# A decoder's latent attention: ScalarE copies each group of turned probabilities one step later

## Chip, cores and metric

The kernel runs on one core of one Trainium2 chip. The metric is the device time of one execution in microseconds (us); less is better. Engines: TensorE (PE; its weight loads are PEld), VectorE (DVE), ScalarE (ACT), GpSimd (POOL) and SyncE (SP), each with its own queue of instructions, worked in order; they wait for each other by semaphores only.

## What is computed

Two decoder layers on x of 4 x 256 x 256, each of self-attention, cross-attention to a context of 4 x 1601 x 64 and a mixture of experts, with a layer norm behind each. The change is in the second layer's cross-attention ("latent block"), 16 heads on a rotated context:

```python
q_hk = (hidden_q @ Wq.T).reshape(Bv, Sv, H, K)
q_big = jnp.einsum('bshk,hkq->bshq', q_hk, w_kc_q)
q_big = _apply_rope(q_big, ...)            # 192 wide
kv_r = _apply_rope(kv_c, ...)              # 1601 x 64
q_r = jnp.einsum('bshq,hqr->bhsr', q_big, W_qr)
k_r = jnp.einsum('bld,hdr->bhlr', kv_r, W_kr)
scores = jnp.einsum('bhsr,bhlr->bhsl', q_r, k_r)
attn = jax.nn.softmax(scores, axis=-1)
ctx_c = jnp.einsum('bhsl,bld->bhsd', attn, kv_r)
ctx_lat = jnp.einsum('bhsd,hkd->bhsk', ctx_c, w_kc_kv)
out = ctx_lat.transpose(0, 2, 1, 3).reshape(Bv, Sv, H * K) @ Wo.T
```

## The kernel before

`latent_attention` (L2426) works on 64 units, one for each head and batch. A unit has 256 queries in two halves of 128 rows, and 1601 keys. Products keep float32 accuracy by splitting an operand into a `_hi` part (ScalarE rounds it to fp32r) and a `_lo` part (VectorE subtracts `_hi` from the source).

For a unit u the work is:

- `score(u, i, j)`: TensorE scores half i against piece j of the keys (304, 496, 496 and 305 wide) into PSUM bank j. It waits until the exponential of the score before it in that bank is done.
- `maximum(u, i, j)`: VectorE reduces each piece; with the fourth it combines the four (L2698) to the row maximum `e_st`.
- `exponential(u, i, j)`: ScalarE, with sum, to `e_P` (L2631). It waits for the combined maximum of its half.
- `turn(u, g)`: TensorE transposes group g of up to 256 keys (seven groups, the last of 65 keys) from `e_P` into one of two banks. It waits until the lower half of group g - 2 has been taken out.
- `upper_pt(u, g)` on ScalarE (L2646, `e_PT_hi`) and `lower_pt(u, g)` on VectorE (L2713, `e_PT_lo`): the two halves of the turned group. The lower one waits for the upper one. These are the copies of the change.
- `attend(u, g)`: TensorE multiplies both halves by the context. `keep_context` (L2638, `e_cx_hi`) copies the result, VectorE its lower half; `project_out` gives the output.

The units are pipelined. Iteration i has eight steps; in step s the engines do, for u = i: score, maximum and exponential of (u, half 1, piece s) or, from step 4 on, of the next unit's half 0 (ScalarE's exponentials lag by half a unit: steps 0 to 3 are half 0 of u, steps 4 to 7 half 1); for v = i - 1: `turn(v, s)`, the two copies of group s, and `attend(v, s - 3)`. The order on each queue is written out by hand in loops over i and step: `tensor` (L2583), `scalar` (L2653), `vector` (L2740). Beside these, in fixed steps: the queries of the next unit are absorbed into the keys' space (`absorb_q`, TensorE step 1; `upper_qk` on ScalarE step 2, L2624, `e_qk_hi`); queries are projected (`project_q`, step 3; ScalarE copies them to `x_in` in step 4, L2314, GpSimd rotates them, ScalarE's `upper_z` copies them in step 7, L2320); and in three of four iterations weights of the next head are folded (`fold_q`, `fold_r`, `fold_o`: TensorE step 5, ScalarE's copy step 6, L2298, L2304 or L2308, VectorE's lower half step 6).

`score_bank` are banks 0 to 3, `tb_bank` (turned groups) 4 and 5, the context has 6, all the rest shares bank 7 (`aux`). There are four `e_PT` buffers, used in turn. In `scalar`, the copy stands at the end of each step:

```python
if v is not None and step < GROUPS:
    upper_pt(v, step)
```

Of the kernel before, what the change touches and what calls it, by code (L numbers as in the profile page):

```python
# [54 lines left out]
def decoder(nc, t, out):  # L55
    with ExitStack() as top:
# [159 lines left out]
        def norm_scalar(turns, b, k):  # L216
            act.wait_ge(xt_turned, turns)
            act.copy(XT_hi[:, :, tok(b)], turned_view(k)).then_inc(xt_hi, 1)
# [20 lines left out]
        def scaled_scalar(turns, b, k, at):  # L239
            act.wait_ge(ln_in, 16)  # L240
            act.wait_ge(xt_turned, turns)
            for c in range(DC):
                last = act.activation(XT_hi[:, c, tok(b)], turned_view(k)[:, c, :], ACT.Copy, scale=ln_w[:, at + c:at + c + 1])
            last.then_inc(xt_hi, 1)
# [60 lines left out]
        def enter_scalar(b):  # L305
            act.wait_ge(x_normed, 16 + b + 1)
            act.copy(x_in[:, 2 * b:2 * b + 2, :], X[:, 2 * b:2 * b + 2, :]).then_inc(x_entered, 1)
# [2118 lines left out]
        def latent_attention(latent, before, following):  # L2426
# [8 lines left out]
            GROUPS = -(-KT // 2)  # L2435
# [6 lines left out]
            with ExitStack() as sc:  # L2442
# [20 lines left out]
                def a_unit(i):  # L2463
                    return i if 0 <= i < N else None
# [5 lines left out]
                def keys_of(g):  # L2470

                    return min(2, KT - 2 * g), min(P, CTX - 2 * g * P)
# [141 lines left out]
                def scalar():  # L2614
                    def upper_o(h):
                        if h >= 2:
                            act.wait_ge(*put_out.at(BATCH * (h - 1)))
                        latent.upper_o(h, bank[aux])

                    def upper_qk(m):  # L2620
                        act.wait_ge(*q_absorbed.at(m + 1))
                        if m >= 2:
                            act.wait_ge(*scored.at(8 * (m - 1)))
                        act.copy(qk[m % 2][0][:], bank[aux][:, 0:SEQ]).then_inc(*qk_hi.up())  # L2624

                    def exponential(u, i, j):
                        if i == 0 and j == 0 and u >= 2:
                            act.wait_ge(*turned.at(GROUPS * (u - 1)))
                        act.wait_ge(*maxed.at(2 * u + i + 1))
                        n, s = PIECES[j], st[u % 4]  # L2630
                        act.activation(Pm[u % 2][:, i, STARTS[j]:STARTS[j] + n], bank[score_bank[j]][:, 0:n], ACT.Exp,  # L2631
                                       bias=s[:, i, 4:5], accum_out=s[:, i, j:j + 1]).then_inc(*exped.up())

                    def keep_context(u):
                        act.wait_ge(*attended.at(GROUPS * (u + 1)))
                        if u >= 2:
                            act.wait_ge(*put_out.at(u - 1))
                        act.copy(cx[u % 2][0][:], bank[ctx_bank][:, 0:SEQ]).then_inc(*cx_hi.up())  # L2638

                    def upper_pt(u, g):  # L2640
                        at = GROUPS * u + g
                        n, rows = keys_of(g)
                        act.wait_ge(*turned.at(at + 1))
                        if at >= PT_BUFS:
                            act.wait_ge(*attended.at(at - PT_BUFS + 1))
                        act.copy(PT[at % PT_BUFS][0][0:rows, 0:n, :],  # L2646
                                 bank[tb_bank[at % 2]][0:rows, 0:n * SEQ].rearrange("p (c n) -> p c n", c=n)).then_inc(*pt_hi.up())

                    act.wait_ge(*before)
                    upper_qk(0)  # L2650
                    upper_o(0)
                    latent.upper_z(1)
                    for i in range(N + 3):  # L2653
                        u, v, w, after = a_unit(i), a_unit(i - 1), a_unit(i - 2), a_unit(i + 1)
                        h, quarter = i // BATCH + 1, i % BATCH
                        for step in range(8):
                            half, j = divmod(step, 4)
                            if u is not None:
                                exponential(u, half, j)
                            if step == LAG - 1 and w is not None:  # L2660
                                keep_context(w)
                            if step == 2 and after is not None:
                                upper_qk(after)
                            if step == 4 and i + 2 < N:
                                latent.keep_q(i + 2, bank[aux])
                            if step == 1 and i == N:
                                enter_scalar(0)
                            if step == 6 and h < H and quarter < 3:
                                if quarter == 0:
                                    latent.upper_q(h, bank[aux])  # L2670
                                elif quarter == 1:
                                    latent.upper_r(h, bank[aux])
                                else:
                                    upper_o(h)
                            if v is not None and step < GROUPS:
                                upper_pt(v, step)
                            if step == 3 and i + 2 == BATCH - 1:
                                norm_scalar(12 + BATCH, BATCH - 1, aux)
                            if step == 2 and i == N:
                                scaled_scalar(16 + 1, 0, enter_bank, 0)  # L2680
                            if step == 7 and i + 2 < N:
                                latent.upper_z(i + 2)
# [108 lines left out]
                sync()  # L2791
                tensor()
                scalar()
                vector()
                gpsimd()
# [166 lines left out]
```

## Time and profile before

| | |
|---|---|
| time, median of 3 runs | 1911.38 us (1908.85 to 1916.75) |
| the profiled execution | 1909.03 us, its span 1907.8 us |
| latent block | about 785 to 1600 us of the span |
| TensorE busy, share of the span | 1775.6 us, 93% |
| VectorE, ScalarE, GpSimd busy | 1289.9 (68%), 1086.8 (57%), 685.6 us (36%) |

The span is the time from the first to the last instruction that the profiler saw. Busy time is the time in which an engine had an instruction at work; TensorE's matmuls overlap, so full busy time doesn't mean full throughput. A timeline row gives start, duration, engine, source line, operation, output and inputs; a bracket at its end gives the idle time ahead of it and what ended that. Consecutive instructions of an engine overlap a little, so the distance between starts is shorter than a duration.

### The profile page before, as it was taken

Reading aid. Unit: us, or ns where it says so; the run is one execution under the profiler, and the core shown is the slowest. Engines: PE = TensorE matmul, PEld = TensorE weight load, DVE = VectorE, ACT = ScalarE, POOL = GpSimd, SP = SyncE. Lnnn points to the kernel's source line nnn. Section 1 sums busy time; section 2 is a strip of 40 time slices with the busy share of each in tenths; the row PEclk is TensorE's granted clock in tenths of the full one; section 3 lists DMA queues with packets and bytes.
Section 4 is the critical chain, followed back from the end, with each engine's and each line's share of the span. In section 5 each row is a group of like instructions: output and inputs, shape, how many; then the busy total and the mean of one; then the engine's idle time right before and its main releaser. Section 6 shows DMA issues by size and latency. Waiting matters only on the chain.

```text
span 1907.8 us, 41954 instructions
## 1 busy us (share of the span) xinstructions
PE 1775.6 (93%) x15624; PEld 1478.5 (77%) x15624; DVE 1289.9 (68%) x3463; ACT 1086.8 (57%) x2750; POOL 685.6 (36%) x674
## 2 busy tenths in 40 slices
PE   7999989889998898699999999999999998898995
PEld 5999977646656776599999999999999997774663
DVE  5677657732237665588888888888888888775222
ACT  5776754212223343488888888888888885431221
POOL 5644322232224422443444334433443341213221
PEclk9999999989999999999999999999999999999998
DMA  4000039023247000000000000000000002402323
GB/s 167 23 1 2 1 131 344 23 87 48 45 101 222 3 3 2 22 12 12 12 12 12 29 12 12 12 12 12 12 12 1 1 2 84 193 2 82 48 46 66
DMA packets 51861, 91.69 MB, mean 48 GB/s; under 512 B 4592, under 2 KB 43632, under 8 KB 49232
## 3 DMA queue, kind: packets, MB, share of 16 engines
q1 hardware_dynamic: 42928, 78.16, 12.3%
q0 software_dynamic: 8160, 10.29, 3.5%
q8 instruction: 129, 2.11, 0.5%
q10 hardware_dynamic: 576, 0.56, 0.1%
q14 instruction: 68, 0.56, 0.1%
HBM read 56.13 MB, written 32.87 MB: 47 GB/s over the span
## 4 chain that ended last, share of the span: by engine, by line
PE 73%; DVE 12%; ACT 6%; issue 3%; POOL 2%; DMA 2%; SPq 0%; ACTq 0%; DVEq 0%; POOLq 0%
PE bank L100 60%; PE bank L2546 10%; DVE a_t L703 2%; ACT d_PT L1338 2%; ACT landing L1338 1%; PE bank L1887 1%; PE bank L1159 1%; DVE a_t L700 1%; PE bank L1866 1%; POOL c_rows L1767 1%; POOL g_rows L1767 1%; DVE tiny L133 1%; PE bank L501 1%; DVE d_nm L1426 1%; DVE X L172 0%
## 5 line engine op out<-in xcount | busy, mean ns | idle before, releaser
L2694 DVE TENSOR_REDUCE e_st<-bank 128x1 f32<-128x496 f32 (+2 forms) x512 | 292.0, 571 | 121.7 <-PE bank L100 120.7
L2631 ACT ACTIVATE e_P<-bank,e_st 128x496 f32<-128x496 f32 (+2 forms) x512 | 307.0, 600 | 95.3 <-DVE e_st L2698 93.5
L2713 DVE TENSOR_TENSOR e_PT_lo<-bank,e_PT_hi 128x512 fp32r<-128x512 f32 (+1 forms) x448 | 287.6, 642 | 1.5 <-ACT e_PT_hi L2646 1.4
L2546 PE MATMUL bank<-ident,e_P 128*128 128x128 f32 (+1 forms) x1664 | 258.4, 274 | 4.2 <-DVE e_PT_lo L2713 3.7
L2646 ACT CAST e_PT_hi<-bank 128x512 fp32r<-128x512 f32 (+1 forms) x448 | 248.3, 554 | 10.9 <-PE bank L2546 6.7
L100 PE MATMUL bank<-e_PT_hi,e_kv 128*128 128x256 f32 (+1 forms) x832 | 249.2, 320 | 0.0
L2546 PEld LDWEIGHTS bank<-ident,e_P 128*128 128x128 f32 (+1 forms) x1664 | 195.0, 140 | 31.3 <-issue 26.5
L100 PE MATMUL bank<-e_PT_lo,e_kv 128*128 128x256 f32 (+1 forms) x832 | 215.6, 280 | 0.0
L100 PE MATMUL bank<-e_KT,e_qk_hi 128*128 128x496 f32 (+2 forms) x512 | 198.9, 389 | 7.2 <-ACT e_P L2631 5.7
L100 PE MATMUL bank<-e_KT,e_qk_lo 128*128 128x496 f32 (+2 forms) x512 | 177.0, 346 | 0.0
L100 PEld LDWEIGHTS bank<-e_PT_lo,e_kv 128*128 128x128 f32 (+1 forms) x832 | 158.4, 190 | 2.5
L100 PEld LDWEIGHTS bank<-e_PT_hi,e_kv 128*128 128x128 f32 (+1 forms) x832 | 157.6, 189 | 2.2
L2393 POOL TENSOR_TENSOR e_r<-x_in,e_ropeq 96x512 f32<-96x512 f32 x32 | 41.1, 1284 | 217.5 <-ACT x_in L2314 217.5
L100 PEld LDWEIGHTS bank<-e_KT,e_qk_hi 128*128 128x128 f32 x512 | 95.9, 187 | 29.6 <-ACT e_P L2631 20.1
L2393 POOL TENSOR_TENSOR x_in<-x_in,e_ropeq 96x512 f32<-96x512 f32 x32 | 41.0, 1282 | 205.2 <-ACT x_in L2314 205.2
L100 PE MATMUL bank<-mask_b,ident_b 128*128 128x128 bf16 (+1 forms) x796 | 100.8, 274 | 11.4 <-DVE d_nm L1428 6.9
L2631 ACT ACTIVATION_READ_ACCUMULATOR e_P<-bank,e_st 128x1 f32 x512 | 102.5, 200 | 0.0
L1531 POOL TENSOR_SCALAR_AFFINE_SELECT landing<-landing 128x768 f32<-128x768 f32 x64 | 39.5, 640 | 167.5 <-ACT landing L1338 167.5
L100 PEld LDWEIGHTS bank<-e_KT,e_qk_lo 128*128 128x128 f32 x512 | 96.9, 189 | 0.1
L1338 ACT ACTIVATE d_PT<-bank 128x1536 f32<-128x1536 f32 x32 | 46.4, 1451 | 86.7 <-PE bank L100 86.7
L100 PEld LDWEIGHTS bank<-mask_b,ident_b 128*128 128x128 bf16 x796 | 58.5, 99 | 44.0 <-DVE d_nm L1428 8.6
L1338 ACT ACTIVATE landing<-bank 128x1536 f32<-128x1536 f32 x32 | 46.4, 1450 | 80.7 <-PE bank L100 80.7
(470 smaller groups left out, 4960.1 us busy)
## 6 DMA issues: line engine op xcount, KB each, us to landing
c_wall<-in_c_w SPq DMA_DIRECT2D x8, 1536.0 KB, 19.0
g_wall<-in_g_w SPq DMA_DIRECT2D x8, 1536.0 KB, 19.4
c_rows<-normed SPq DMA_DIRECT2D x9, 1040.0 KB, 12.9
g_rows<-normed SPq DMA_DIRECT2D x9, 1040.0 KB, 13.1
e_stage<-in_e_w SPq DMA_DIRECT2D x16, 416.0 KB, 3.2
c_xs<-c_rows SPq DMA_DIRECT2D x23, 130.0 KB, 2.1
g_xs<-g_rows SPq DMA_DIRECT2D x23, 130.0 KB, 2.1
landing<-in_a_wo SPq DMA_DIRECT2D x2, 1024.0 KB, 6.1
```

Of the source, the lines that this page charges most:

```text
L100: return pe.matmul(o, a, b, start=start, stop=stop, skip_group_check=True)
L133: stats = dve.bn_stats(T[:, 6 * i:6 * i + 6], X[:, 2 * b + i, :])
L703: last = dve.tensor_tensor(b_[o:o + 64], src[i:i + 64], sin, ALU.mult)
L1338: act.activation(PT[n % 2].rearrange("p a j n -> p (a j n)"), psum[:, B_BANK:B_BANK + 3, :].rearrange("p a n -> p (a n)"), ACT.Exp, scale= ...
L1531: last = pool.affine_select(blocks, blocks, pattern=pattern, compare_op=ALU.is_ge, fill=0.0, base=0, channel_multiplier=-1)
L1767: pool.indirect_dma_start(scratch[self.name][0][:, :], bass.IndirectOffsetOnAxis(ap=self.slots[:, n, k:k + 1], axis=0), self.payload[:, n, ...
L2393: pool.tensor_tensor(x1, v, self.ropeq[:, 0:2, :], ALU.mult)
L2546: last = pe.transpose(o[0:rows, c * SEQ + i * P:c * SEQ + (i + 1) * P], p[:, i, k0:k0 + rows], ident[:])
L2631: act.activation(Pm[u % 2][:, i, STARTS[j]:STARTS[j] + n], bank[score_bank[j]][:, 0:n], ACT.Exp, bias=s[:, i, 4:5], accum_out=s[:, i, j:j ...
L2646: act.copy(PT[at % PT_BUFS][0][0:rows, 0:n, :], bank[tb_bank[at % 2]][0:rows, 0:n * SEQ].rearrange("p (c n) -> p c n", c=n)).then_inc(*pt_ ...
L2694: last = dve.tensor_reduce(s[:, i, j:j + 1], bank[score_bank[j]][:, 0:PIECES[j]], AX.X, ALU.max)
L2713: dve.tensor_tensor(lo, bank[tb_bank[at % 2]][0:rows, 0:n * SEQ].rearrange("p (c n) -> p c n", c=n), hi.bitcast(F32), ALU.subtract).then_i ...
```

## The change

A table `PT_BEHIND` names, for each step, the groups that ScalarE copies at its end. Step 0 and step 4 now copy none, steps 1 and 2 the group before (0 and 1), step 3 groups 2 and 3, steps 5, 6 and 7 groups 4, 5 and 6. No other engine's order is touched.

```diff
+                    PT_BEHIND = ((), (0,), (1,), (2, 3), (), (4,), (5,), (6,))
+
                     act.wait_ge(*before)
...
-                            if v is not None and step < GROUPS:
-                                upper_pt(v, step)
+                            for g in PT_BEHIND[step] if v is not None else ():
+                                upper_pt(v, g)
```

ScalarE, steps 0 to 3 of an iteration (there `e_P1` is the unit's exponentials, and groups 0 to 3 of the unit before go to `e_PT0` to `e_PT3`). Before:

```order
L2631 ACTIVATE e_P1,e_st1<-bank,e_st1 128x304
L2646 CAST e_PT0_hi<-bank 128x512
L2631 ACTIVATE e_P1,e_st1<-bank,e_st1 128x496
L2646 CAST e_PT1_hi<-bank 128x512
L2631 ACTIVATE e_P1,e_st1<-bank,e_st1 128x496
L2638 CAST e_cx1_hi<-bank 128x256
L2624 CAST e_qk0_hi<-bank 128x256
L2646 CAST e_PT2_hi<-bank 128x512
L2631 ACTIVATE e_P1,e_st1<-bank,e_st1 128x305
L2646 CAST e_PT3_hi<-bank 128x512
```

and with the change:

```order
L2631 ACTIVATE e_P1,e_st1<-bank,e_st1 128x304
L2631 ACTIVATE e_P1,e_st1<-bank,e_st1 128x496
L2646 CAST e_PT0_hi<-bank 128x512
L2631 ACTIVATE e_P1,e_st1<-bank,e_st1 128x496
L2638 CAST e_cx1_hi<-bank 128x256
L2624 CAST e_qk0_hi<-bank 128x256
L2646 CAST e_PT1_hi<-bank 128x512
L2631 ACTIVATE e_P1,e_st1<-bank,e_st1 128x305
L2646 CAST e_PT2_hi<-bank 128x512
L2646 CAST e_PT3_hi<-bank 128x512
```

Group 0 moves behind the second exponential, group 1 behind the third and behind the copies of context and `qk`, group 2 behind the fourth.

ScalarE, steps 4 to 7 of the same iteration (groups 4 to 6 go to `e_PT0` to `e_PT2`; `e_w2_hi0` is the copy of the folded weights). Before:

```order
L2631 ACTIVATE e_P1,e_st1<-bank,e_st1 128x304
L2314 COPY x_in<-bank 96x512
L2646 CAST e_PT0_hi<-bank 128x512
L2631 ACTIVATE e_P1,e_st1<-bank,e_st1 128x496
L2646 CAST e_PT1_hi<-bank 128x512
L2631 ACTIVATE e_P1,e_st1<-bank,e_st1 128x496
L2304 CAST e_w2_hi0<-bank 96x256
L2646 CAST e_PT2_hi<-bank 65x256
L2631 ACTIVATE e_P1,e_st1<-bank,e_st1 128x305
L2320 CAST e_qr_hi1<-e_r1 96x512
```

and with the change:

```order
L2631 ACTIVATE e_P1,e_st1<-bank,e_st1 128x304
L2314 COPY x_in<-bank 96x512
L2631 ACTIVATE e_P1,e_st1<-bank,e_st1 128x496
L2646 CAST e_PT0_hi<-bank 128x512
L2631 ACTIVATE e_P1,e_st1<-bank,e_st1 128x496
L2304 CAST e_w2_hi0<-bank 96x256
L2646 CAST e_PT1_hi<-bank 128x512
L2631 ACTIVATE e_P1,e_st1<-bank,e_st1 128x305
L2646 CAST e_PT2_hi<-bank 65x256
L2320 CAST e_qr_hi1<-e_r1 96x512
```

Group 4 moves behind the second exponential, group 5 behind the third and the copy of the folded weights, group 6 behind the fourth.

VectorE, steps 0 to 3 of the same iteration (lines are those of the changed kernel, two higher than before):

```order
L2696 TENSOR_REDUCE e_st1<-bank 128x1
L2715 TENSOR_TENSOR e_PT0_lo<-bank,e_PT0_hi 128x512
L2696 TENSOR_REDUCE e_st1<-bank 128x1
L2715 TENSOR_TENSOR e_PT1_lo<-bank,e_PT1_hi 128x512
L2720 TENSOR_TENSOR e_cx1_lo<-bank,e_cx1_hi 128x256
L2690 TENSOR_TENSOR e_qk0_lo<-bank,e_qk0_hi 128x256
L2696 TENSOR_REDUCE e_st1<-bank 128x1
L2715 TENSOR_TENSOR e_PT2_lo<-bank,e_PT2_hi 128x512
```

This order is the same before and with the change: the lower half of group 1 stands ahead of those of context and `qk`.

## Rows read from the trace of the kernel before

**Rows 1.** Windows: length, busy us of PE, PEld, DVE, ACT, POOL; granted clock, DMA.

```profile
600.00:785.00 185.00, 161.58 (x2784) 126.71 (x2784) 114.70 (x248) 72.75 (x95) 74.26 (x87) 0.98 0.05 16
785.00:1600.00 815.00, 802.30 (x5938) 737.62 (x5935) 684.95 (x1661) 652.05 (x1750) 320.96 (x307) 0.99 0.04 10
```

**Rows 2.** Waits, 900 to 1500 us: waiting <- waited for, us, times, longest.

```profile
DVE e_st L2694 <- PE bank L100: 84.4, 201, 0.7
ACT e_P L2631 <- DVE e_st L2698: 70.6, 83, 1.0
```

**Rows 3.** Lines by form, latent block: busy, mean ns | idle before, releasers.

```profile
L100 PEld LDWEIGHTS bank<-e_KT,e_qk_hi 128*128 128x128 f32 x500 | 93.7, 187 | 22.3 <-ACT e_P L2631 14.4 <-issue 0.3
```

**Rows 4.** Timeline of ScalarE, steps 0 to 3 of one iteration.

```profile
1201.64 0.52 ACT L2631 ACTIVATE e_P<-bank,e_st 128x304 f32<-128x304 f32 x1 [0.69 <-DVE e_st L2698]
...
1202.15 0.58 ACT L2646 CAST e_PT_hi<-bank 128x512 fp32r<-128x512 f32 x1
1202.61 0.69 ACT L2631 ACTIVATE e_P<-bank,e_st 128x496 f32<-128x496 f32 x1
...
1203.33 0.59 ACT L2646 CAST e_PT_hi<-bank 128x512 fp32r<-128x512 f32 x1
1203.81 0.68 ACT L2631 ACTIVATE e_P<-bank,e_st 128x496 f32<-128x496 f32 x1
...
1204.47 0.37 ACT L2638 CAST e_cx_hi<-bank 128x256 fp32r<-128x256 f32 x1
1204.92 0.37 ACT L2624 CAST e_qk_hi<-bank 128x256 fp32r<-128x256 f32 x1
1205.36 0.59 ACT L2646 CAST e_PT_hi<-bank 128x512 fp32r<-128x512 f32 x1
```

**Rows 5.** Timeline of VectorE, the same steps.

```profile
1204.20 0.67 DVE L2694 TENSOR_REDUCE e_st<-bank 128x1 f32<-128x496 f32 x1 [0.23 <-PE bank L100]
1204.79 0.68 DVE L2713 TENSOR_TENSOR e_PT_lo<-bank,e_PT_hi 128x512 fp32r<-128x512 f32 x1
...
1207.73 0.16 DVE L2698 TENSOR_REDUCE e_st<-e_st 128x1 f32<-128x4 f32 x1
```

**Rows 6.** Timeline of TensorE, the same steps.

```profile
1203.44 0.50 PE L100 MATMUL bank<-e_KT,e_qk_hi 128*128 128x496 f32 x1
1203.78 0.39 PE L100 MATMUL bank<-e_KT,e_qk_lo 128*128 128x496 f32 x1
...
1204.60 0.28 PE L100 MATMUL bank<-e_qr_hi,e_w_lo 96*128 96x256 f32 x1
...
1205.62 0.63 PE L2546 MATMUL bank<-ident,e_P 128*128 128x128 f32 x4
```

**Rows 7.** Timeline of ScalarE, steps 4 to 6 of the same iteration.

```profile
1207.92 0.52 ACT L2631 ACTIVATE e_P<-bank,e_st 128x304 f32<-128x304 f32 x1 [1.00 <-DVE e_st L2698]
...
1210.61 0.68 ACT L2631 ACTIVATE e_P<-bank,e_st 128x496 f32<-128x496 f32 x1
...
1211.66 0.37 ACT L2304 CAST e_w_hi<-bank 96x256 fp32r<-96x256 f32 x1 [0.28 <-PE bank L100]
1212.03 0.37 ACT L2646 CAST e_PT_hi<-bank 65x256 fp32r<-65x256 f32 x1
```

**Rows 8.** Timeline of VectorE, from group 5 to the combined maximum.

```profile
1211.65 0.68 DVE L2713 TENSOR_TENSOR e_PT_lo<-bank,e_PT_hi 128x512 fp32r<-128x512 f32 x1
1212.25 0.41 DVE L2345 TENSOR_TENSOR e_w_lo<-bank,e_w_hi 96x256 fp32r<-96x256 f32 x1
1212.94 0.67 DVE L2694 TENSOR_REDUCE e_st<-bank 128x1 f32<-128x496 f32 x1 [0.29 <-PE bank L100]
1213.54 0.41 DVE L2713 TENSOR_TENSOR e_PT_lo<-bank,e_PT_hi 65x256 fp32r<-65x256 f32 x1
...
1214.36 0.16 DVE L2698 TENSOR_REDUCE e_st<-e_st 128x1 f32<-128x4 f32 x1
```

**Rows 9.** Timeline of ScalarE, the `wq` fold's copy one iteration earlier.

```profile
1198.82 0.48 ACT L2298 CAST e_wq_hi<-bank 128x384 fp32r<-128x384 f32 x1 [0.33 <-PE bank L100]
```

## The prediction

> **What bounds the kernel now.** I read the page first, then the stage of the change by windows, then who waits for whom, then one iteration of the loop engine by engine. By the page TensorE is busy for 93% of the span, VectorE for 68%, ScalarE for 57% (table above). The latent block runs from about 785 to 1600 us, 64 units, so 12.7 us each; there TensorE is busy 802 of 815 us, VectorE 685, ScalarE 652 [rows 1]. So TensorE bounds the stage, and a change on ScalarE counts only by the waits that it takes from TensorE or gives to it. The waits [rows 2] show a ring: VectorE's maxima wait for TensorE (84.4 us in 600), the exponentials wait for the combined maximum of VectorE (70.6), and the weight loads of TensorE's scores wait for an exponential to free a bank (14.4 us in the stage) [rows 3]. Each of the three is only just in time for the next.
>
> One iteration shows where. It is the one that starts at 1201.24, with a fold of the `w2` weights in its step 5; times below without a date are us after 1200. ScalarE: exponential 0 at 1.64, copy of group 0 at 2.15, exponential 1 at 2.61, copy 1 at 3.33, exponential 2 at 3.81, context 4.47, `qk` 4.92, copy 2 at 5.36 [rows 4]. VectorE, whose order doesn't change, takes the lower half of group 1 at 4.79, right behind the maximum that it began at 4.20, and goes on without a gap to the combined maximum at 7.73 [rows 5]. TensorE turns group 3 at 5.62 [rows 6]: that needs the bank that the lower half of group 1 empties at 4.79 + 0.68 = 5.47. This path has no slack: group 3 is turned 0.15 us after its bank is free. VectorE's lower half of a group can't start before ScalarE's copy of the same group, so the question is when the copies of groups 1 and 5, which end early today, come to stand behind something that ends late.
>
> **The change part by part.** No instruction is added or removed; on ScalarE six of seven copies in each unit stand behind one more exponential, with what follows it (group 3 stays in its step). DMA, SyncE and GpSimd issue nothing else and are passed by nothing; the GpSimd rotation hangs on the `x_in` copy of step 4, which keeps its place behind exponential 4 and moves with it.
>
> *Exponential 1 earlier.* It follows exponential 0 directly: 2.15 in place of 2.61. TensorE's score of step 1 began at 3.44, behind that exponential's end at 2.61 + 0.69 = 3.30, and lasted 0.50 us where its second half, unhindered, lasted 0.39 [rows 6]. That and the wait ahead of it give back an estimated 0.19 us in the iteration; over the stage, the weight loads ahead of such scores stood idle for exponentials for 14.4 us, with the one of step 0, which doesn't change [rows 3]. That is all the good that I find.
>
> *Copy 1 behind context and `qk`: the first wait.* ScalarE now: exponential 0 1.64, exponential 1 2.15, copy 0 2.86, exponential 2 3.34, context 4.00 (between starts 0.51, about 0.70 and 0.66 us for exponentials, 0.48 for a copy) [rows 4]. The `qk` copy waits for TensorE's absorption, which ended at 4.60 + 0.28 = 4.88 and now ends 0.19 earlier: so `qk` at 4.73, where today it stood at 4.92. Copy 1 follows 0.44 later (as 4.92 to 5.36 today): 5.17, and ends 0.59 later, 5.76. Today it ended at 3.92. VectorE is through with its maximum by 4.70 and then stands behind copy 1 until 5.80, in place of 4.79: **+1.01 us**. Behind it are queued the lower halves of context and `qk`, two maxima, group 2 and the combination; they had no gap, so the combined maximum comes at 7.73 + 1.01 = 8.74. TensorE can't use the time: its next bank comes at 5.80 + 0.68, so group 3 is turned at 6.63, also 1.01 late, and all that follows in order with it. Copies 2 and 3 fall into the 1.00 us in which ScalarE waited for the maximum anyway [rows 7], and cost nothing; without that cover they would cost 0.96.
>
> *Copy 5 behind the fold's copy: the second wait.* Exponential 4 at 7.92 + 1.01 = 8.93. Up to exponential 6 one copy fewer stands between (10.61 - 7.92 = 2.69, less 0.48): 11.14, done at 11.81. Next is the copy of the folded weights, which waits for TensorE: 11.66 + 1.01 = 12.67 [rows 7]. Copy 5, which today goes out ahead of exponential 6, follows at 12.67 + 0.37 = 13.04 and ends at 13.63. VectorE's lower half of group 5 was at 11.65, would be at 12.66 by the first wait alone, and comes at 13.67: another 1.01. From there to the combined maximum VectorE took 2.71 us with a gap of 0.29 and small slack around it [rows 8]; without any it takes 0.60 + 0.33 + 0.60 + 0.82 = 2.35. So the combination is at 16.02 against 14.36: the next exponential 0, and with it the next iteration, is **1.66 us** late. Copy 6 (ready by 14.41) is in time for its lower half at 15.2 and costs nothing.
>
> *The other kinds of iteration*, worked the same way: the fold of `wq` has a copy of 0.48 us where that of `w2` takes 0.37 and begins it later in its step [rows 9], its lower half is as much longer, and VectorE has no gap there to make up with: 2.06. The fold of `wo` is like `w2`, 1.65. The quarter of iterations without a fold has no second wait; only copy 4, which now ends at 11.14 + 0.11 = 11.25, makes its lower half and the turning of group 6 a little late: 1.25. These three are estimates by the steps above. The mean is (1.66 + 2.06 + 1.65 + 1.25) / 4 = 1.66 us.
>
> *Bounds of the unknown.* No row shows VectorE standing behind a copy this long, so how much of the second wait stays is the open size: at least nothing of it (1.01 us), at most the value of the `wq` iteration in all (2.1 us). I take 1.66, since it follows from rows of the very instructions.
>
> *Sum.* 63 iterations have both exponentials and copies: 63 x 1.66 = 104.6 us. Against the profiled execution (1909.03 us, of which 1907.8 are the span) that gives 2013.6, so **2013 us**; the median of the runs is 2.35 us above the profiled execution, which I leave inside the range. TensorE's own work is unchanged; it would idle for an eighth of the stage.
>
> **The rivals.**
>
> A. *Only the first wait counts*: TensorE, itself late, gives ScalarE time, and the second hides. For it: VectorE still has gaps before its maxima, which begin behind TensorE's scores (84.4 us in 600, so 1.8 us an iteration) [rows 2]. Against it: the copy of the fold waits for TensorE, so it shifts with it. 63 x 1.01 = 64 us: 1973.
>
> B. *Faster*: the one mechanism is exponential 1, which goes ahead of copy 0 and frees the bank of the second piece. It decides if VectorE finds copy 1 done when it wants it, at 4.79; then TensorE saves up to the 14.4 us [rows 3]: 1895. Against it: copy 1 would have to start by 4.20, and exponential 2, context and `qk` stand ahead of it.
>
> C. *No change*: VectorE's gaps of 1.8 us an iteration swallow a wait of 1.01. For it the size; against it that the gaps lie behind waits for TensorE, which is held by the very same late lower half. 1911.
>
> D. *TensorE's clock falls*, since TensorE would idle by about 0.9 us at group 3 and again at the head of each iteration. The rows speak against it: in 600 to 785 us TensorE was busy 161.58 of 185 us, 87%, about what I forecast for the stage, and the granted clock was 0.98, so at the 2.4 GHz level nearly throughout [rows 1]. If it ran at 1.2 GHz in one iteration of ten, the 12.7 us of each of six iterations would double: 76 us on top, 2090. The Trainium skill (TensorE: Matmul & The Clock Gate, "The HAM clock gate") has the half rate as the default and activity as what releases it; by that rule alone the idle time added here would count against the clock. The trace bears out that 87% still held it.
>
> That the table doesn't do what it says can be left out: the order of ScalarE's instructions shows it.
>
> **How the numbers follow.** The forecast has 0.74, A 0.13, B 0.04, C 0.03, D 0.03, and 0.03 is for waits that add up above the upper bound. The range of the forecast case goes up to 63 x 2.1 = 132 us, 2041, and is widened a little for the median; down it reaches to A. So 1970 to 2045. Within 0.5% (what a measurement can tell from no change) lies C alone; faster is B; the rest is slower by far more than that.
>
> **What would show it.** In the profile after: VectorE's lower half of a group waiting for ScalarE's copy (`e_PT_lo` behind `e_PT_hi`), hardly there today, at the top of the waits with some 1 us once or twice an iteration, 60 to 120 us in all; TensorE's weight loads of a turning idle until `e_PT_lo`; the wait of step 1's score for exponential 1 gone; TensorE's busy time unchanged in work but some 88% of a stage of about 920 us; the granted clock still near 1. I am wrong if VectorE doesn't wait for group 1, or if ScalarE's `qk` copy comes well ahead of 4.7 us in its iteration; the second wait is wrong if iterations with and without a fold grow alike.

## The result and the profile after

| | before | with the change |
|---|---|---|
| time, median | 1914.07 us | 1998.37 us |
| all runs | 1908.85 to 1923.89 | 1996.58 to 2003.45 |
| profiled execution (span) | 1909.03 (1907.8) | 2003.45 (2002.2) |

The ratio is 1.0438, with a 95% interval of 1.039 to 1.0487: 84 us slower. The range of 1970 to 2045 held it; the 2013 forecast is 15 us too high.

The costliest groups of the page after show the forecast's mark at once. In each line: busy, mean ns of one, then the idle time ahead of it and what ended that.

```profile
L2715 DVE TENSOR_TENSOR e_PT_lo<-bank,e_PT_hi 128x512 fp32r<-128x512 f32 (+1 forms) x448 | 289.9, 647 | 104.6 <-ACT e_PT_hi L2646 95.9
...
L2546 PE MATMUL bank<-ident,e_P 128*128 128x128 f32 (+1 forms) x1664 | 258.8, 275 | 61.0 <-DVE e_PT_lo L2715 59.5
```

The same two lines of the page before:

```profile
L2713 DVE TENSOR_TENSOR e_PT_lo<-bank,e_PT_hi 128x512 fp32r<-128x512 f32 (+1 forms) x448 | 287.6, 642 | 1.5 <-ACT e_PT_hi L2646 1.4
L2546 PE MATMUL bank<-ident,e_P 128*128 128x128 f32 (+1 forms) x1664 | 258.4, 274 | 4.2 <-DVE e_PT_lo L2713 3.7
```

VectorE's idle time for these copies went from 1.4 to 95.9 us, TensorE's ahead of the turnings from 3.7 to 59.5, and the mean durations are the same within 1%. So these instructions got no longer; the engines stand.

The view of the tile `e_PT_lo` after counts how often: 109 waits. One for group 1 in each of 63 iterations leaves 46, and 44 iterations have both a fold and copies.

```profile
L2715 DVE TENSOR_TENSOR e_PT_lo<-bank,e_PT_hi x448: 408/690/693, 793.5 to 1693.8; 128x512 fp32r<-128x512 f32 x128, 65x256 fp32r<-65x256 f32 x22
...
  ACT e_PT_hi L2646: 95.9, 109
```

The waits after, 900 to 1500 us (waiting, waited for, us in all, times, longest), answer to [rows 2]:

```profile
DVE e_PT_lo L2715 <- ACT e_PT_hi L2646: 66.9, 75, 1.0
PEld bank L2546 <- ACT e_P L2631: 59.2, 53, 1.3
DVE e_st L2696 <- PE bank L100: 48.7, 85, 0.7
ACT e_P L2631 <- DVE e_st L2700: 48.2, 54, 1.1
```

The first line was not among the waits before. VectorE's maxima wait less for TensorE than before (48.7 against 84.4 us), since VectorE is late itself. The second line is the weight load of a turning and is put down to an exponential that was done long before; the matmul behind it names the true releaser, `e_PT_lo`.

The windows of the latent block and of 600 to 785 us answer to [rows 1] (length, busy us of PE, PEld, DVE, ACT, POOL; granted clock, DMA):

```profile
600.00:785.00 185.00, 163.02 (x2793) 127.16 (x2792) 113.69 (x248) 70.77 (x86) 71.66 (x84) 0.95 0.07 19
790.00:1695.00 905.00, 819.04 (x5962) 737.98 (x5962) 701.49 (x1671) 642.07 (x1754) 321.87 (x307) 0.99 0.03 9
```

TensorE is busy 819 of 905 us, 90.5%, where it was 98.4%, and the clock stayed at 0.99 in the block. Ahead of the block, where nothing is changed, it was 0.95 in this execution against 0.98.

Now the iteration of [rows 4 to 8], with the fold of `w2`, in the trace after. It is the one that starts at 1252.26. ScalarE:

```profile
1252.91 0.51 ACT L2631 ACTIVATE e_P<-bank,e_st 128x304 f32<-128x304 f32 x1 [1.49 <-PE bank L2546]
...
1253.41 0.67 ACT L2631 ACTIVATE e_P<-bank,e_st 128x496 f32<-128x496 f32 x1
...
1254.06 0.58 ACT L2646 CAST e_PT_hi<-bank 128x512 fp32r<-128x512 f32 x1
1254.53 0.70 ACT L2631 ACTIVATE e_P<-bank,e_st 128x496 f32<-128x496 f32 x1
...
1255.19 0.39 ACT L2638 CAST e_cx_hi<-bank 128x256 fp32r<-128x256 f32 x1
1256.00 0.37 ACT L2624 CAST e_qk_hi<-bank 128x256 fp32r<-128x256 f32 x1 [0.42 <-PE bank L100]
1256.27 0.59 ACT L2646 CAST e_PT_hi<-bank 128x512 fp32r<-128x512 f32 x1
...
1263.72 0.37 ACT L2304 CAST e_w_hi<-bank 96x256 fp32r<-96x256 f32 x1 [0.77 <-PE bank L100]
1263.99 0.59 ACT L2646 CAST e_PT_hi<-bank 128x512 fp32r<-128x512 f32 x1
...
1267.21 0.52 ACT L2631 ACTIVATE e_P<-bank,e_st 128x304 f32<-128x304 f32 x1 [1.31 <-PE bank L2546]
```

Both copies stand right behind a copy that waited for TensorE: `qk` 0.42 us, the fold's 0.77 us. The wait of the first and last row is put down to a turning; VectorE's combination ended at 1252.66 + 0.16, just ahead of the exponential. VectorE and TensorE of the same iteration:

```profile
1256.89 0.69 DVE L2715 TENSOR_TENSOR e_PT_lo<-bank,e_PT_hi 128x512 fp32r<-128x512 f32 x1 [0.94 <-ACT e_PT_hi L2646]
...
1259.84 0.16 DVE L2700 TENSOR_REDUCE e_st<-e_st 128x1 f32<-128x4 f32 x1
...
1264.61 0.69 DVE L2715 TENSOR_TENSOR e_PT_lo<-bank,e_PT_hi 128x512 fp32r<-128x512 f32 x1 [0.82 <-ACT e_PT_hi L2646]
...
1266.96 0.16 DVE L2700 TENSOR_REDUCE e_st<-e_st 128x1 f32<-128x4 f32 x1
```

```profile
1257.73 0.63 PE L2546 MATMUL bank<-ident,e_P 128*128 128x128 f32 x4 [0.87 <-DVE e_PT_lo L2715]
```

VectorE stands 0.94 us for the copy of group 1 and 0.82 us for that of group 5. TensorE stands 0.87 us before it can turn group 3. The second wait reaches it by another way: VectorE's combined maximum is late, so exponential 0 is late, and the score of step 0 waits for that exponential. There TensorE stands only a little:

```profile
1267.87 0.41 PE L100 MATMUL bank<-e_KT,e_qk_hi 128*128 128x304 f32 x1 [0.24 <-ACT e_P L2631]
```

From exponential 0 to exponential 0 this iteration takes 67.21 - 52.91 = 14.30 us against 12.97 before.

### The profile page after: what moved, and what is told of

Its sections match the earlier page's. It is cut to its first block, busy times and chain, and to the rows that moved or that the text cites. A ratio compares the mean times of both kernels' runs of the same rounds, so it can differ in the third digit from the quotient of the medians.

```text
span 2002.2 us, 41954 instructions
## 1 busy us (share of the span) xinstructions
PE 1800.9 (90%) x15624; PEld 1485.0 (74%) x15624; DVE 1301.9 (65%) x3463; ACT 1076.1 (54%) x2750; POOL 686.5 (34%) x674
## 4 chain that ended last, share of the span: by engine, by line
PE 67%; DVE 15%; ACT 9%; issue 5%; DMA 2%; POOL 2%; SPq 0%; ACTq 0%; DVEq 0%; POOLq 0%
PE bank L100 55%; PE bank L2546 8%; DVE e_PT_lo L2715 3%; ACT e_PT_hi L2646 2%; DVE a_t L703 2%; ACT d_PT L1338 2%; ACT landing L1338 1%; PE bank L1159 1%; PE bank L1887 1%; ACT e_P L2631 1%; DVE a_t L700 1%; PE bank L1866 1%; DVE tiny L133 1%; PE bank L501 0%; DVE X L172 0%
## 5 line engine op out<-in xcount | busy, mean ns | idle before, releaser
L2715 DVE TENSOR_TENSOR e_PT_lo<-bank,e_PT_hi 128x512 fp32r<-128x512 f32 (+1 forms) x448 | 289.9, 647 | 104.6 <-ACT e_PT_hi L2646 95.9
L2546 PE MATMUL bank<-ident,e_P 128*128 128x128 f32 (+1 forms) x1664 | 258.8, 275 | 61.0 <-DVE e_PT_lo L2715 59.5
L2646 ACT CAST e_PT_hi<-bank 128x512 fp32r<-128x512 f32 (+1 forms) x448 | 249.5, 557 | 38.1 <-PE bank L2546 38.1
L100 PE MATMUL bank<-e_KT,e_qk_hi 128*128 128x496 f32 (+2 forms) x512 | 193.6, 378 | 17.2 <-ACT e_P L2631 16.0
L100 PEld LDWEIGHTS bank<-e_KT,e_qk_lo 128*128 128x128 f32 x512 | 97.5, 190 | 0.1
```

The lines of the kernel that those rows point to most:

```text
L100: return pe.matmul(o, a, b, start=start, stop=stop, skip_group_check=True)
L2546: last = pe.transpose(o[0:rows, c * SEQ + i * P:c * SEQ + (i + 1) * P], p[:, i, k0:k0 + rows], ident[:])
L2646: act.copy(PT[at % PT_BUFS][0][0:rows, 0:n, :], bank[tb_bank[at % 2]][0:rows, 0:n * SEQ].rearrange("p (c n) -> p c n", c=n)).then_inc(*pt_ ...
L2715: dve.tensor_tensor(lo, bank[tb_bank[at % 2]][0:rows, 0:n * SEQ].rearrange("p (c n) -> p c n", c=n), hi.bitcast(F32), ALU.subtract).then_i ...
```

## The experiments

All are compared with the kernel before, run beside them on the same chip. Its median was 1915.62 us beside the two halves, the copies ahead of what waits for TensorE, and the moved lower half of group 1; 1914.12 beside group 4, the gain alone and the lower half of group 6; 1912.91 beside the run between context and `qk` and the first half with copy 1 ahead. It was 1914.07 beside the change. So two runs are compared by their distances to it.

The traces give a second measure, one execution of each kernel: the time from the first turning of the latent block to the last, and the length of an iteration from exponential 0 to the next, as the median of its kind. Before and with the change the turnings run as follows:

```profile
L2546 PE MATMUL bank<-ident,e_P x1664: 270/272/418, 784.6 to 1601.3; 128*128 128x128 f32 x171, 128*65 128x128 f32 x14
```

```profile
L2546 PE MATMUL bank<-ident,e_P x1664: 270/272/446, 790.7 to 1693.1; 128*128 128x128 f32 x171, 128*65 128x128 f32 x14
```

That is 816.7 and 902.4 us. Outside this stretch, where nothing differs, the profiled executions took 1091 to 1103 us, so differences of some 10 us between single executions are read from the stretch and not from the whole. All numbers in the table are differences to the kernel before, in us; its iterations take 12.97, 12.66, 12.88 and 12.30:

| kernel | median time | turnings | `w2` fold | `wo` fold | `wq` fold | no fold |
|---|---|---|---|---|---|---|
| the change | +84.3 | +85.7 | +1.32 | +1.49 | +1.70 | +0.99 |
| first half | +48.9 | +51.2 | +0.79 | +0.77 | +0.79 | +0.80 |
| second half | +34.8 | +34.8 | +0.52 | +0.72 | +0.92 | +0.18 |
| second half, group 4 in its place | +32.3 | +33.0 | +0.52 | +0.72 | +0.91 | -0.01 |
| copies ahead, steps 2 and 6 | -13.9 | -11.3 | -0.24 | -0.26 | -0.23 | -0.05 |
| first half, copy 1 between context and `qk` | -1.4 | +0.6 | 0.00 | -0.03 | +0.01 | +0.01 |
| change, lower half of group 1 later | +85.0 | +85.7 | +1.33 | +1.50 | +1.70 | +0.98 |
| exponential 1 ahead of copy 0 | -7.6 | -12.3 | -0.19 | -0.21 | -0.19 | -0.18 |
| first half, copy 1 ahead | -15.5 | -13.9 | -0.24 | -0.24 | -0.23 | -0.23 |
| copies ahead, lower half of group 6 later | -18.7 | -20.3 | -0.39 | -0.39 | -0.38 | -0.21 |
| lower half of group 6 later | -7.5 | -8.0 | -0.17 | -0.17 | -0.14 | -0.16 |

**The first half alone, and the second half alone.** The theory was two waits that add up; the rival, that one hides in the other.

```diff
-PT_BEHIND = ((), (0,), (1,), (2, 3), (), (4,), (5,), (6,))
+PT_BEHIND = ((), (0,), (1,), (2, 3), (4,), (5,), (6,), ())     # first half
+PT_BEHIND = ((0,), (1,), (2,), (3,), (), (4,), (5,), (6,))     # second half
```

> Groups 0 to 3 as in the change, groups 4 to 6 in their old places. Theory (two waits of VectorE for ScalarE's copies, group 1 behind the qk copy and group 5 behind the fold's copy, that add up): only the first one, by the profile after 0.84 us an iteration, so 63 x 0.84 = 53 us more than before. Rival (one wait is enough to make the other appear, the second hides in the first): the full difference of about 84 us. Rival (the fold's copy is all that matters): within 10 us of before.

> Groups 4 to 6 as in the change, groups 0 to 3 in their old places. Theory of two waits that add up: the lower half of group 5 comes 0.9 us late in iterations with a fold, 0.36 of that is made up by VectorE's gaps: 0.5 to 0.75 us in 47 iterations and some 0.15 in 16 without one, 25 to 35 us more than before, and with the first half alone about the whole change. Rival (second wait hides unless the first is there): within 5 us of before.

Measured: 1964.55 us for the first half, ratio 1.0252 (1.0222 to 1.0281), 49 us above before; 1950.45 us for the second, ratio 1.0181 (1.0151 to 1.0212), 35 us above. Together 84 us, the whole change. The line of VectorE's lower halves on the page of each, first half and then second half:

```profile
L2715 DVE TENSOR_TENSOR e_PT_lo<-bank,e_PT_hi 128x512 fp32r<-128x512 f32 (+1 forms) x448 | 288.7, 645 | 62.8 <-ACT e_PT_hi L2646 59.6
```

```profile
L2715 DVE TENSOR_TENSOR e_PT_lo<-bank,e_PT_hi 128x512 fp32r<-128x512 f32 (+1 forms) x448 | 288.4, 644 | 43.1 <-ACT e_PT_hi L2646 37.9
```

The idle times add up as well: 59.6 + 37.9 = 97.5 us against 95.9 in the change. So does the time of each kind of iteration, within 0.01 us (`wq` fold: 0.79 + 0.92 against 1.70). The rivals are out. The second expectation counted 47 iterations with a fold and 16 without; there are 44 and 19.

The two halves reach TensorE by different ways. The line of TensorE's turnings on each page, first half and then second half:

```profile
L2546 PE MATMUL bank<-ident,e_P 128*128 128x128 f32 (+1 forms) x1664 | 259.2, 275 | 59.9 <-DVE e_PT_lo L2715 59.5
```

```profile
L2546 PE MATMUL bank<-ident,e_P 128*128 128x128 f32 (+1 forms) x1664 | 258.3, 274 | 6.6 <-DVE e_PT_lo L2715 4.8
```

Nearly all of TensorE's wait for lower halves comes from the first half (before, it was 3.7 us). The second half's loss goes through the combined maximum and exponential 0, as read above in one iteration; no run changes that way alone, so it is read from traces and not shown by an experiment.

**Group 4 left in its place**, in the second half's change:

```diff
+PT_BEHIND = ((0,), (1,), (2,), (3,), (4,), (), (5,), (6,))
```

> The second half's change without that of group 4: groups 0 to 4 in their old places, 5 behind the fold's copy, 6 behind its exponential. Theory: the wait for copy 5 stays (47 iterations with a fold), the loss of the iterations without a fold (0.44 us each in the run of the whole second half) goes, since it is the turning of group 6 that waits for group 4: some 7 us less than the whole second half, so 25 to 30 us above before. Rival (group 4 is the main part): 15 us or less above before.

Measured: 1946.45 us, ratio 1.018 (1.0153 to 1.0208), 32 us above before, 2.5 us nearer to it than the whole second half. The intervals don't tell these two apart, but the traces do by kind: in iterations without a fold the loss of 0.18 us is gone, in all others it stays. 0.18 us in 19 iterations are 3.4 us, where the expectation had 0.44 us each and 7 in all. The wait for the copy of group 5 is the second half's cost; group 4 is a small part.

**Copies behind the exponential, but ahead of what waits for TensorE.** In steps 2 and 6 the copy comes directly behind the exponential:

```diff
                             if u is not None:
                                 exponential(u, half, j)
+                            for g in PT_BEHIND[step] if v is not None and step in (2, 6) else ():
+                                upper_pt(v, g)
...
-                            for g in PT_BEHIND[step] if v is not None else ():
+                            for g in PT_BEHIND[step] if v is not None and step not in (2, 6) else ():
```

> The change, but in steps 2 and 6 the copy of the group stands directly behind the exponential, ahead of context, qk and the fold's copy. Theory: both waits are gone, since copy 1 ends at 4.6 us in its iteration and VectorE wants it at 4.7; what stays is exponential 1 ahead of copy 0, which gives TensorE 0.19 us an iteration: 5 to 14 us less than before (1900 to 1909 if before is at 1914). Rival (a copy behind one more exponential is late by itself, whatever stands between): 40 us or more above before.

Measured: 1901.73 us, ratio 0.9925 (0.9897 to 0.9953): 14 us less than before, some 98 below the change. All seven groups are copied in the very steps of the change; only their place against the context, `qk` and fold copies differs. The whole loss hangs on that place, and behind it a gain comes to light. The rival, that one step later is late by itself, is out.

**Between context and `qk`.** The first half's change again, with copy 1 behind the context copy and ahead of `qk`:

```diff
                                 keep_context(w)
+                            if step == 2 and v is not None:
+                                upper_pt(v, 1)
                             if step == 2 and after is not None:
                                 upper_qk(after)
...
+                            for g in PT_BEHIND[step] if v is not None and step != 2 else ():
```

> The first half's change (groups 0 to 3), with copy 1 between the copies of context and qk instead of behind both. Theory: it is qk's wait for TensorE's absorption that holds copy 1 back, not the work of the two copies; copy 1 then ends near 5.0 us in its iteration, the turning of group 3 comes some 0.2 to 0.3 us late, less the 0.13 that exponential 1 gives: 0 to 15 us above before, where the first half had 49. Rival (each operation ahead of copy 1 costs its own time): half of it, 25 us above before.

Measured: 1911.5 us, ratio 0.9995 (0.9983 to 1.0007). Moving one copy ahead of one other takes the 49 us of the first half to nothing, and the rival is out. ScalarE in one iteration of this run:

```profile
1245.71 0.69 ACT L2631 ACTIVATE e_P<-bank,e_st 128x496 f32<-128x496 f32 x1
...
1246.37 0.39 ACT L2638 CAST e_cx_hi<-bank 128x256 fp32r<-128x256 f32 x1
1246.62 0.62 ACT L2646 CAST e_PT_hi<-bank 128x512 fp32r<-128x512 f32 x1
1247.16 0.37 ACT L2624 CAST e_qk_hi<-bank 128x256 fp32r<-128x256 f32 x1
```

Copy 1 starts 0.91 us behind the start of exponential 2, in the change 1.74 (1254.53 to 1256.27). Of these 0.83 us the `qk` copy's own work is 0.27 (1256.00 to 1256.27) and its wait the rest, so over 63 iterations about 17 us are work and 35 are wait, by estimate: the wait is the greater part and not all of it. Work ahead of copy 1 isn't free either, as the context copy shows further below. Some of TensorE's wait is left and eats the gain of exponential 1: the weight loads of the turnings, which in 900 to 1500 us of the kernel before had stood 15.3 us without a releaser, now have this line beside 3.4 of that kind:

```profile
PEld bank L2546 <- ACT e_P L2631: 22.6, 47, 0.5
```

**Which engine's queue pays.** In the change, VectorE takes the lower half of group 1 behind those of context and `qk`, so that they don't stand behind its wait:

```diff
                             if step == 2 and after is not None:
                                 lower_qk(after)
+                            if step == 2 and v is not None:
+                                lower_pt(v, 1)
...
-                            if v is not None and step < GROUPS:
+                            if v is not None and step < GROUPS and step != 1:
                                 lower_pt(v, step)
```

> The change, but VectorE takes the lower half of group 1 behind those of context and qk, so they don't stand behind its wait. Theory A (TensorE's bank decides: the turning of group 3 waits for this lower half, which copy 1 holds back anyway): at most 0.2 us an iteration are back, 0 to 15 us less than the change. Theory B (the work queued on VectorE behind the wait decides): 0.66 us an iteration are back, some 40 us less than the change, 1955 to 1960.

Measured: 2000.65 us, ratio 1.0439 (1.0406 to 1.0472), as the change. The two lines of its page:

```profile
L2715 DVE TENSOR_TENSOR e_PT_lo<-bank,e_PT_hi 128x512 fp32r<-128x512 f32 (+1 forms) x448 | 290.0, 648 | 50.5 <-ACT e_PT_hi L2646 38.1
...
L2546 PE MATMUL bank<-ident,e_P 128*128 128x128 f32 (+1 forms) x1664 | 258.8, 275 | 60.9 <-DVE e_PT_lo L2715 59.2
```

VectorE's wait for copies fell from 95.9 to 38.1 us, and the time didn't move, for TensorE's wait is 59.2 us as before. Much of the 58 us only changed its name. VectorE's maxima, now early, wait longer for TensorE's scores, 118.4 us where it was 83.0 in the change (the lines on the pages, change first):

```profile
L2696 DVE TENSOR_REDUCE e_st<-bank 128x1 f32<-128x496 f32 (+2 forms) x512 | 290.7, 568 | 92.1 <-PE bank L100 83.0
```

```profile
L2696 DVE TENSOR_REDUCE e_st<-bank 128x1 f32<-128x496 f32 (+2 forms) x512 | 291.5, 570 | 127.4 <-PE bank L100 118.4
```

What decides in the first half is the bank that TensorE needs for group 3, and the work queued behind VectorE's wait is not the bound. Theory A holds, though of the up to 15 us that it allowed none came back.

**The gain alone.** The kernel before with exponential 1 ahead of copy 0:

```diff
+PT_BEHIND = ((), (0, 1), (2,), (3,), (4,), (5,), (6,), ())
```

> The kernel before with one thing of the change alone: exponential 1 stands ahead of copy 0, all else in its old place. Theory: this is the whole gain of the run with the copies ahead of context, qk and fold, 8 to 14 us less than before. Rival (that gain came from the later copies 2, 4, 5 or 6): within 4 us of before.

Measured: 1906.49 us, ratio 0.9954 (0.9937 to 0.997), 8 us less than before, just short of the 8 to 14 expected. The swap is a gain by itself, and in the trace every kind of iteration is 0.18 to 0.21 us shorter, 12.3 us over the block. Lines by form of its latent block: the first matmul of each score of 496 columns has a mean of 410 ns, where the same line of the kernel before has 435.

```profile
L100 PE MATMUL bank<-e_KT,e_qk_hi 128*128 128x496 f32 x252 | 103.3, 410 | 0.7 <-ACT e_P L2631 0.7
```

Then the first half with copy 1 directly behind its exponential (step 2 only, groups 4 to 6 in their old places):

> Copies of the first half behind one more exponential and copy 1 directly behind it, ahead of context and qk; second half as before. Theory: no wait of the change is left, exponential 1 gives its gain, 8 to 14 us less than before. If the rest of the gain of the run with both halves (14 against 9 us of the swap alone) comes from the second half, this is at 1905; if from the first, at 1901.

Measured: 1897.39 us, ratio 0.992 (0.99 to 0.9939), 16 us less than before, a little more than was expected of either case, and level with the run that moves both halves. So the second half gives nothing; without a fold it costs 0.18 us, as group 4 did above. Whether this is better than the swap alone stays open: the two intervals just touch, and the turnings differ by 1.6 us. Against the run between context and `qk`, on the same chip, copy 1 stands ahead of one 128x256 copy more; it starts 0.24 us earlier behind exponential 2 (1248.41 to 1249.08, so 0.67 us), and the time is 14 us less. So the context copy's own work costs 14 us where it stands ahead of copy 1.

**One more wait of the ring.** The combined maximum stands behind VectorE's lower half of group 6. This kernel is the one with copies ahead in steps 2 and 6, and takes that half behind the combination; the other does so in the kernel before:

```diff
-                            if v is not None and step < GROUPS:
-                                lower_pt(v, step)
+                            if v is not None and step != 6:
+                                lower_pt(v, min(step, 6))
```

> The copies directly behind the exponential in steps 2 and 6, and on VectorE the lower half of group 6 behind the last maximum of the unit and the combination. Theory: the combination, and with it exponential 0 and the score of step 0, come up to 0.17 us earlier, and TensorE's wait of step 0 (16 us over the stage in all) shrinks: 5 to 12 us less than the same kernel without it, about 1890 to 1897. Rival (the maximum waits for TensorE as long as the lower half took): no difference, 1902.

> The kernel before with VectorE's lower half of group 6 behind the last maximum and the combination, nothing else. Theory: 5 to 12 us less than before. Rival: no difference.

Measured: 1895.41 us, ratio 0.9907 (0.9886 to 0.9928), for the first; 1906.6 us, ratio 0.9967 (0.9954 to 0.9981), for the second. The step in the kernel before is a gain by its interval. On top of the copies ahead the two intervals overlap (0.9886 to 0.9928 and 0.9897 to 0.9953); there the trace speaks for it, with turnings 9.0 us shorter, as the step alone gives 8.0. The first kernel beats both kernels of this study: 19 us below before, some 103 below the change. Moving the lower half of group 6 alone took TensorE's wait for exponentials ahead of scores, 9.1 us in 900 to 1500 before, down to this line:

```profile
PEld bank L100 <- ACT e_P L2631: 0.2, 1, 0.2
```

## Why the prediction was right, and by how much it was off

*What bounds the stage.* Right. The ring of three waits of [rows 2, 3] had little slack, and the two places named were the ones that broke. The forecast's "0.9 us at group 3 and again at the head of each iteration" for TensorE is right for group 3 (0.87) and not for the head (0.24).

*Exponential 1 earlier.* Right. 0.19 us an iteration would be 12 us; the swap alone gave 0.18 to 0.21 us in each kind of iteration and 12.3 over the turnings, and 8 by the medians. One reading beside it was wrong: the weight loads' wait of 14.4 us [rows 3] holds nothing of step 1. In 900 to 1500 us it is 9.3 us with the swap and was 9.1 before, and 0.2 with the lower half of group 6 moved. So it is the wait of step 0.

*The first wait.* The mechanism was right and the size a little high. From exponential 0, the lower half of group 1 was to come at 5.80 - 1.64 = 4.16 us and came at 56.89 - 52.91 = 3.98. Before it was 4.79 - 1.64 = 3.15, so the wait costs 0.83 us and not 1.01. Exponentials 1 and 2 and copy 0 are within 0.08 us of the forecast and `qk` is where it was expected (3.09 us from exponential 0 in both); the difference arises behind `qk`. The sum took 0.44 us from `qk` to the next copy, as 4.92 to 5.36 in [rows 4], and it is 0.27 (56.00 to 56.27). Those 0.44 us were no pace of ScalarE: copy 2, at 1205.36, was waiting there for its turning, which TensorE ended at 1204.71 + 0.60 = 1205.31:

```profile
1204.71 0.60 PE L2546 MATMUL bank<-ident,e_P 128*128 128x128 f32 x4
```

The term that was mis-sized is this: **a distance between two starts was read as the time of an operation, although the second one was waiting.** The row of copy 2 shows no idle time: the distance was still short, since the `qk` copy itself lasted until 1205.29.

*Why the iteration is late.* I gave two reasons for it, VectorE's queue without a gap and TensorE's bank. For the first wait, the run with the lower half moved shows that the bank suffices; relieving VectorE's queue was worth nothing there. The forecast said that TensorE could not use the time, and this was the half that counted. For the second wait it is VectorE's queue, as far as the traces of the two halves show it; no run tests that.

*The second wait.* The mechanism was right and the size again a little high, for the same reason: 0.37 us from the fold's copy to the next one [rows 7] was 0.27 (63.72 to 63.99), for copy 6 there waited for its turning too (TensorE ended it at 1211.98, the copy began at 1212.03). From exponential 0 the lower half of group 5 was to come at 12.03 and came at 11.70; before, 10.01. So the two waits cost 1.69 us up to there and not 2.02; the two copies make 0.27 of these 0.33. Behind it, VectorE's way to the combination was forecast as 2.35 us without a gap, and it is 66.96 - 64.61 = 2.35.

*Sum.* This iteration takes 14.30 us, against 14.63 forecast. By kind the forecast was high everywhere: 1.66, 1.65, 2.06 and 1.25 us for `w2`, `wo`, `wq` and no fold, against 1.32, 1.49, 1.70 and 0.99. The `wq` fold lost the most and no fold the least, as forecast. So iterations with and without a fold didn't grow alike, the sign that would have spoken against the second wait. The turnings take 85.7 us more, or 1.36 us for each of 63 iterations where the sum had 1.66. (The sum also gave the iterations without a fold a quarter; they are 19 of 63, which is worth 2 us.) The other 8.7 us of the 94.4 between the two spans lie outside the block, 6.1 of them ahead of it, where no instruction differs; by the medians the change costs 84.

*Rivals.* A had the first wait alone: that kernel costs 49 us, not 64, and the second wait was not hidden. B was wrong as a forecast, but its mechanism exists and is worth 8 us by the medians, 12 by the turnings, though not out of the 14.4 us that it named: its condition, VectorE finding copy 1 done when it wants it, is what the run with the copies ahead sets up, and that kernel is faster. C is out: VectorE's gaps did shrink (84.4 to 48.7 us in 600) and swallowed nothing, as TensorE stood too. D is out: the granted clock was 0.99 in the block with TensorE 90.5% busy, so at the 2.4 GHz level. By the Trainium skill (TensorE: Matmul & The Clock Gate, "The HAM clock gate") idle time speaks for the lower rate; in this trace, with waits of 0.87 and 0.24 us in an iteration of 14.30, it didn't come to that.

## What to carry to other kernels

When a copy is moved in a hand-written order, look at what it now stands behind: behind work it costs that work once its slack is gone (14 us here for a copy of 0.25 us in each iteration), and behind an operation that itself waits for a third engine it inherits the wait as well. Let the operation that another engine needs next go ahead of the one that waits, even within the same step; here one such exchange was the difference between 49 us lost and none. And before an interval between two starts goes into a sum, see whether the second one was waiting, for back-to-back operations overlap and hide a short wait from the profile's idle column.

## What was not expected

Taking 58 us of waiting for copies away from VectorE changed the time by nothing, and 35 us of it came back as waiting for TensorE: an idle column says where an engine stands, not what its standing costs. And a copy of 128x256 held ScalarE for 0.25 to 0.27 us up to the next start, with a duration of 0.37 to 0.39, where the next one was ready; the longer distances behind it that are read here, 0.44, 0.45 and 0.81 us, were waits for TensorE.
